# Frame axes read from a PSUM bank, three-term sums by tensor_reduce, and features stored component by component in a graph network's tensor product

## The chip, the core and the metric

The kernel runs on one core of a Trainium2 chip. The metric is the device time of one execution in microseconds (us); lower is better. Before the change the median of three runs is 9208.38 us (9191.51 to 9210.93).

## What is computed

Two message-passing layers run over one graph of 12,500 nodes and 400,000 edges (sorted by destination). The first is an attention layer with 4 heads. The second, which the change touches, is a tensor product. Each node has 32 features: 8 scalars and 8 vectors of 3 components.

```python
h = jnp.maximum(_layernorm(x, axis=-1), 0.0)
x = x + _L0_gnn_ref(h, Wq, Wk, Wv, Wo, edge_index)         # attention over edges
h = jnp.maximum(_layernorm(x, axis=-1), 0.0)
x = x + _L1_gnn_ref(h, edge_weight, edge_attr_3, edge_index, w1, b1, w2, b2)
# inside _L1_gnn_ref
R = jax.nn.relu(abs_distances[:, None] @ w1 + b1) @ w2 + b2   # 64 hidden units
Fj = features[src]                                            # one row of 32 per edge
acc = acc + _NORM[i] * jnp.einsum('euv,ef,evi,ofi->euo', Rb[..., k], Yf, Fb, C)
out = out.at[dst].add(msg)
```

## The kernel before

The kernel does not form the spherical harmonics. For each edge it keeps a frame: 3 axes of 3 numbers, the first along the edge. The three vector components of the gathered features are rotated into this frame, the radial products are formed there, and the result is rotated back.

The edges lie as 128 partitions by 3,132 slots. `tensor_product` walks over them in 58 chunks of T = 54 slots (`CHUNKS`, `T`), two buffers by turns. A chunk is cut into 9 steps (`SPC`, index s). The five engines run hand-written queues, tied by semaphores.

- GpSimd (POOL) issues 54 indirect DMAs for each chunk (L909). Each fetches 128 rows of `h2` (printed as `scratch_h`) into `feat[b]`. Its queue holds nothing else. It waits for `feat_free`, and two buffers are free at the start.
- TensorE makes the radial weights in `psR` (L924 and L925, six PSUM banks) and adds up the products over j by identity matmuls into `psS` (L935 and L938, two banks by turns). In its queue the radial matmuls of step s + 1 stand ahead of the sums of step s.
- VectorE (DVE) runs the order written in `body`: in step s come `products` (two instructions, L1181), then the pieces listed in `before` (of the last chunk's `finish`) and `ahead` (of the next chunk's `components`), then in steps 2, 5 and 8 a `split` (L1144), then `fold` (L1190).
- ScalarE (ACT) moves each step's sums from `psS` to `red` (L1027), and between those it does the hidden layer, copies of the scalars, the flags and the output.
- SyncE (SP) loads weights, stacked halves and frames.

```python
before = {1: (0, 1), 2: (2,), 3: (3, 4), 4: (5, 6)}
ahead = {5: (0,), 6: (1, 2), 7: (3,), 8: (4,)}
```

`components` rotates in. Its parts 0 to 2 multiply `feat` (vector components at steps of 3 words) by the frame (L1155, 1,296 elements each). Parts 3 and 4 add the three terms in two instructions (L1166 and L1168). Part 0 is where VectorE waits for a chunk's features. `finish` rotates back: three products (L1198), one addition (L1206), one addition that writes the transposed `seed` (L1210), and two scans along the edges (L1219). Ahead of the tensor product, `node_attention` writes `h2`; after it, `node_sums` gathers the sums of the nodes (L1292) and adds them to `x` (L1324). The first layer, `attention`, has a gather loop of the same make (L483), with its running state in PSUM tiles.

## Time and profile before

| what | value |
|---|---|
| median of three runs | 9208.38 us (9191.51 to 9210.93) |
| the profiled execution | 9176.9 us, its span 9175.1 us |
| busy, TensorE / VectorE / ScalarE / GpSimd | 42% / 55% / 21% / 75% of the span |
| stage of the tensor product | from about 4414 us to about 9035 us |

A busy share is an average over stages; the second half of the span, from about 4414 us, is the stage that is changed. In it TensorE and VectorE are busier than these shares say. A printed duration is from start to end; where instructions of VectorE follow each other at once, each starts about 0.08 us before the printed end of the one ahead.

### The profile page before, as it was taken

The numbers are of one execution on the slowest core, as the hardware profiler recorded it, in microseconds if no ns is written. First come the engines' busy times: TensorE is split into PE (matmuls) and PEld (weight loads), VectorE is DVE, ScalarE is ACT, GpSimd is POOL, SyncE is SP. The second block draws the span as 40 slices with busy tenths as digits, with TensorE's granted clock in tenths as the row PEclk, the third lists the DMA queues.
The fourth block names the chain that finished last, engine by engine and source line by source line (L and its number), as shares of the span: only waits on it lengthen the run. The fifth ranks groups of instructions, "written<-read, shape, count | busy, mean of one in ns | idle before, by whom it ended". The sixth has DMA issues, their size and how long they took to land. (4 is left out here: it accounts for less than half of the span.)

```text
span 9175.1 us, 70106 instructions
## 1 busy us (share of the span) xinstructions
PE 3812.2 (42%) x20406; PEld 2991.3 (33%) x20406; DVE 5008.3 (55%) x4743; ACT 1961.5 (21%) x1940; POOL 6926.4 (75%) x6677
## 2 busy tenths in 40 slices
PE   1000000000000000000388888888888888888883
PEld 0000000000000000000266666666666666666662
DVE  3133333333333333332477777777777777777773
ACT  0021221212212112121122222222222222222220
POOL 6777777777777777776777777777777777777774
PEclk6555555555555555555699999999999999999996
DMA  7122222222222222221233333333333333333331
GB/s 284 39 65 57 62 63 60 65 57 62 63 58 67 57 62 63 58 66 38 65 84 83 80 84 81 84 84 84 80 82 85 85 84 82 80 84 84 83 79 29
DMA packets 416998, 691.52 MB, mean 75 GB/s; under 512 B 170350, under 2 KB 247902, under 8 KB 405070
## 3 DMA queue, kind: packets, MB, share of 16 engines
q1 hardware_dynamic: 174376, 356.79, 14.4%
q0 software_dynamic: 213216, 166.16, 11.1%
q10 hardware_dynamic: 29382, 168.33, 4.5%
q14 instruction: 19, 0.16, 0.0%
q8 instruction: 5, 0.08, 0.0%
HBM read 345.81 MB, written 190.98 MB: 59 GB/s over the span
## 5 line engine op out<-in xcount | busy, mean ns | idle before, releaser
L909 POOL DMA_INDIRECT feat<-scratch_h,src x3132 | 3557.5, 1136 | 973.1 <-issue 954.2
L483 POOL DMA_INDIRECT kv<-scratch_kv,src_i x3132 | 2961.8, 946 | 968.0 <-issue 954.2
L935 PE MATMUL psS<-prod,ident 128*128 128x192 f32 x11136 | 1895.0, 326 | 0.0
L1181 DVE TENSOR_TENSOR prod<-psR,ops 128x1536 f32<-128x1536 f32 x1044 | 1784.6, 1752 | 148.4 <-PE psR L925 138.4
L935 PEld LDWEIGHTS psS<-prod,ident 128*128 128x128 f32 x11136 | 1838.6, 190 | 75.1 <-DVE prod L1181 0.3
L700 PE MATMUL psA<-ident,tail 128*36 128x128 f32 x3 | 0.8, 413 | 4098.9 <-DVEq L725 4098.9
L700 PEld LDWEIGHTS psA<-ident,tail 128*36 128x36 f32 x3 | 0.3, 128 | 4099.5 <-DVEq L725 4099.5
L924 PE MATMUL psR<-whigh,stack 128*128 128x512 f16 x3132 | 1227.9, 392 | 54.0 <-DVE prod L1181 36.3
L925 PE MATMUL psR<-wlow,capped 128*128 128x512 f16 x3132 | 1221.2, 390 | 0.0
L589 DVE TENSOR_TENSOR qk<-psQ,kv 128x1728 f32<-128x1728 f32 x58 | 113.5, 1957 | 2017.8 <-DMA kv<-scratch_kv,src_i 2017.8
L1027 ACT ACTIVATE red<-psS,scales 128x192 f32<-128x192 f32 x522 | 219.4, 420 | 3350.0 <-PE psS L938 3350.0
L938 PE MATMUL psS<-prod,ident 128*128 128x192 f32 x2784 | 603.3, 354 | 767.2 <-DVE prod L1190 767.2
L1155 DVE TENSOR_TENSOR parts<-feat,frame 128x1296 f32<-128x1296 f32 x174 | 329.8, 1924 | 923.8 <-DMA feat<-scratch_h,src 923.8
L938 PEld LDWEIGHTS psS<-prod,ident 128*128 128x128 f32 x2784 | 511.2, 207 | 784.0 <-DVE prod L1190 784.0
L509 ACT ACTIVATE psD<-decay 128x1980 f32<-128x1980 f32 x58 | 107.4, 1851 | 2588.6 <-DVEq L600 2588.6
L924 PEld LDWEIGHTS psR<-whigh,stack 128*128 128x128 f16 x3132 | 316.8, 101 | 398.2 <-issue 61.0
L925 PEld LDWEIGHTS psR<-wlow,capped 128*128 128x128 f16 x3132 | 315.4, 101 | 364.3 <-issue 46.4
L1190 DVE TENSOR_TENSOR prod<-prod 128x576 f32<-128x576 f32 x522 | 357.1, 684 | 2.2
L516 ACT ACTIVATE out<-sums 128x1944 f32<-128x1944 f32 x58 | 220.2, 3796 | 462.6 <-DVEq L608 462.6
L603 DVE TENSOR_TENSOR ev<-kv,psQ 128x1728 f32<-128x1728 f32 x58 | 178.2, 3072 | 151.3 <-ACT psQ L513 151.3
L1198 DVE TENSOR_TENSOR parts<-red,frame 128x1296 f32<-128x1296 f32 x174 | 256.9, 1503 | 6.2 <-ACT red L1027 6.2
L607 DVE TENSOR_TENSOR_SCAN sums<-psD,ev 128x1980 f32<-128x1980 f32 x58 | 248.3, 4281 | 2.0
(250 smaller groups left out, 3863.8 us busy)
## 6 DMA issues: line engine op xcount, KB each, us to landing
units<-in_wT SPq DMA_DIRECT2D x348, 288.0 KB, 4.6
scratch_state<-out ACTq DMA_DIRECT2D x58, 1080.0 KB
scratch_qexp<-zeros ACTq DMA_DIRECT2D x32, 1566.0 KB, 43.9
kv<-scratch_kv,src_i POOLq DMA_INDIRECT x3132
qin<-scratch_qexp SPq DMA_DIRECT2D x58, 864.0 KB, 4.6
feat<-scratch_h,src POOLq DMA_INDIRECT x3132
stack<-high SPq DMA_DIRECT2D x348, 144.0 KB
stack<-low SPq DMA_DIRECT2D x348, 144.0 KB
```

What stands on the lines that cost most here:

```text
L483: nc.gpsimd.indirect_dma_start(kv[b][:, t, :], None, a["kv"], bass.IndirectOffsetOnAxis(ap=src_i[b][:, t:t + 1].bitcast(U32), axis=0)).the ...
L516: nc.scalar.activation(out[b][:, :, 0:SUMS], sums[:, :, 1:T1].rearrange("p c t -> p t c"), ACT.Copy).then_inc(sums_copied, 1)
L607: step(v.tensor_tensor_scan(flat(sums), flat(decay_c), ev[:, :, :, :].rearrange("p h c t -> p (h c t)"), 0.0, ALU.mult, ALU.add))
L909: nc.gpsimd.indirect_dma_start(feat[b][:, t, :], None, a["h2"], bass.IndirectOffsetOnAxis(ap=src_i[b][:, t:t + 1].bitcast(U32), axis=0)).t ...
L924: nc.tensor.matmul(psR[:, g % 2, t, :], stack[:, slot, at:at + P], whigh[:, :], start=True, stop=False)
L925: last_mm = nc.tensor.matmul(psR[:, g % 2, t, :], capped[:, slot, at:at + P], wlow[:, :], start=False, stop=True)
L935: nc.tensor.matmul(psS[:, r, 0:GC].rearrange("p (x u) -> p x u", u=VU), ident[:, :], prod[r][:, :, j, :], start=(n == 0), stop=False)
L938: last_mm = nc.tensor.matmul(psS[:, r, 0:GC].rearrange("p (x u) -> p x u", u=VU), ident[:, :], prod[r][:, :, j, :], start=False, stop=(j = ...
L1155: step(v.tensor_tensor(parts[:, :, n, :].rearrange("p t (i v) -> p t i v", i=3), feat[b][:, :, VU:D].rearrange("p t (v i) -> p t i v", i=3 ...
L1181: v.tensor_tensor(prod[r][:, half * TRI * KINDS:(half + 1) * TRI * KINDS, :, :], psR[:, g % 2, :, :].rearrange("p t (x j u) -> p (t x) j u ...
L1190: v.tensor_tensor(prod[r][:, :, 0:FOLDS[s], :], prod[r][:, :, 0:FOLDS[s], :], prod[r][:, :, JC // 2:JC // 2 + FOLDS[s], :], ALU.add).then_ ...
L1198: step(v.tensor_tensor(parts[:, :, n, :].rearrange("p t (o u) -> p t o u", o=3), red[b][:, :, (n + 1) * VU:(n + 2) * VU].rearrange("p t (o ...
```

## The change

1. In `tensor_product`, ScalarE copies the frame of a chunk into a PSUM bank `psF` (486 elements) before each use: once for `components` (after the step-4 move of sums) and once for `finish` (after the step-0 move). VectorE reads the frame from there, and two semaphores (`axes_ready`, `axes_read`) hand the bank back and forth. The bank is taken from `psS`, which has one bank instead of two; TensorE's sums of a step now wait until ScalarE has moved those of the step ahead.
2. The three terms are added by `tensor_reduce`: in `components` three of them (1,296 elements read, 432 written each) in place of L1166 and L1168, in `finish` one (3,888 read, 1,296 written) in place of L1206 and L1210.
3. The vector features are stored component by component (i, then u) in `h2`, the sums and `state2`. `node_attention` makes a turned copy of its features for that, and `node_sums` adds in two instructions, one of them with a turned reading.

```diff
-        hs = sb("hs3", [P, BLOCKS, D])
+        hs, turned_hs = sb("hs3", [P, BLOCKS, D]), sb("turned_hs3", [P, BLOCKS, D])
...
-                                 hs[:, b0:b0 + blocks_of(i), :]).then_inc(h_stored, 16)
+                                 turned_hs[:, b0:b0 + blocks_of(i), :]).then_inc(h_stored, 16)
...
+                    step(v.tensor_copy(turned_hs[:, at, 0:VU], hs[:, at, 0:VU]))
+                    step(v.tensor_copy(turned_hs[:, at, VU:D].rearrange("p b (i u) -> p b u i", i=3),
+                                       hs[:, at, VU:D].rearrange("p b (u i) -> p b u i", i=3)))
...
-        psS = pb("psS", [P, 2, 512])
+        psS = pb("psS", [P, 512])
+        psF = pb("psF", [P, 512])
+        axes = psF[:, 0:9 * T].rearrange("p (t n i) -> p t n i", n=3, i=3)
...
+        axes_ready, axes_read = sem("axes_ready"), sem("axes_read")
...
-                    pe.wait_ge(sum_free, q + 1)
+                    pe.wait_ge(sum_free, q + 2)
...
+                def show_axes(b, copies, last_use):
+
+                    act.wait_ge(axes_read, copies)
+                    nc.scalar.activation(psF[:, 0:9 * T], frame[b][:, :, :].rearrange("p t c -> p (t c)"), ACT.Copy).then_inc(axes_ready, 1)
+                    if last_use:
+                        act.wait_ge(axes_ready, copies + 1)
+                        act.sem_inc(frame_free, 1)
...
+                act.wait_ge(frame_here[0], 16)
+                nc.scalar.activation(psF[:, 0:9 * T], frame[0][:, :, :].rearrange("p t c -> p (t c)"), ACT.Copy).then_inc(axes_ready, 1)
...
                             if s == 0 and not (first and b == 0):
+                                show_axes(1 - b, c * 2, True)
                                 seed_scalars(1 - b, c - 1)
+                            if s == 4 and more:
+                                act.wait_ge(frame_here[1 - b], (c + b) * 8 + 16)
+                                show_axes(1 - b, c * 2 + 1, False)
                             if s == 5 and not (first and b == 0):
                                 store(c - 1, at - T)
                             if s == 5:
...
+                show_axes(1, CHUNKS * 2 - 1, True)
                 seed_scalars(1, CHUNKS - 1)
...
-                def components(step, b, c, n):
-
+                def components(step, b, c, n, copies):
+
+                    def add_up(n):
+                        return v.tensor_reduce(ops[b][:, :, n + 1, VU:JC], parts[:, :, n, :].rearrange("p t (i u) -> p t u i", i=3), axis=AX.X, op=ALU.add)
                     if n < 3:
                         if n == 0:
                             vec.wait_ge(feat_here[b], (c - b) * (8 * T) + 16 * T)
-                            vec.wait_ge(frame_here[b], (c - b) * 8 + 16)
-                        step(v.tensor_tensor(parts[:, :, n, :].rearrange("p t (i v) -> p t i v", i=3),
-                                             feat[b][:, :, VU:D].rearrange("p t (v i) -> p t i v", i=3),
-                                             frame[b][:, :, 3 * n:3 * n + 3].rearrange("p t (i o) -> p t i o", o=1).to_broadcast([P, T, 3, VU]), ALU.mult), hold=False)
+                            vec.wait_ge(axes_ready, copies)
+                        step(v.tensor_tensor(parts[:, :, n, :].rearrange("p t (i u) -> p t i u", i=3),
+                                             feat[b][:, :, VU:D].rearrange("p t (i u) -> p t i u", i=3),
+                                             axes[:, :, n, :].rearrange("p t (i o) -> p t i o", o=1).to_broadcast([P, T, 3, VU]), ALU.mult), hold=False)
                         return
                     step.settle()
                     if n == 3:
+                        vec.sem_inc(axes_read, 1)
                         vec.wait_ge(ops_copied, c + 1)
                         vec.sem_inc(feat_free, 1)
-                    term = lambda i: parts[:, :, :, i * VU:(i + 1) * VU]
-                    to = ops[b][:, :, 1:KINDS, VU:JC]
-                    if n == 3:
-                        step(v.tensor_tensor(term(0), term(0), term(1), ALU.add), hold=False)
+                        step(add_up(0), hold=False)
+                        step(add_up(1), hold=False)
                     else:
-                        v.tensor_tensor(to, term(0), term(2), ALU.add).then_inc(turned_ready, 1)
+                        add_up(2).then_inc(turned_ready, 1)
...
-                def finish(step, b, c, n):
+                def finish(step, b, c, n, copies):

                     flat = lambda x, lo, hi: x[:, lo:hi, :].rearrange("p c t -> p (c t)")
                     if n < 3:
                         if n == 0:
                             vec.wait_ge(sum_free, c * SPC + SPC + 2)
+                            vec.wait_ge(axes_ready, copies)
                         step(v.tensor_tensor(parts[:, :, n, :].rearrange("p t (o u) -> p t o u", o=3),
                                              red[b][:, :, (n + 1) * VU:(n + 2) * VU].rearrange("p t (o u) -> p t o u", o=1).to_broadcast([P, T, 3, VU]),
-                                             frame[b][:, :, 3 * n:3 * n + 3].rearrange("p t (i o) -> p t i o", o=1).to_broadcast([P, T, 3, VU]), ALU.mult), hold=False)
+                                             axes[:, :, n, :].rearrange("p t (i o) -> p t i o", o=1).to_broadcast([P, T, 3, VU]), ALU.mult), hold=False)
                         return
                     step.settle()
                     if n == 3:
-                        vec.sem_inc(frame_free, 1)
+                        vec.sem_inc(axes_read, 1)
                         vec.sem_inc(red_free, 1)
-                        step(v.tensor_tensor(parts[:, :, 0, :], parts[:, :, 0, :], parts[:, :, 1, :], ALU.add), hold=False)
                     elif n == 4:
                         vec.wait_ge(scanned, c * 2 + 1)
                         step(v.tensor_copy(seed[:, :, 0], run[:, :, T]), hold=False)
-                        step(v.tensor_tensor(seed[:, VU:D, 1:T1].rearrange("p (u o) t -> p t o u", o=3),
-                                             parts[:, :, 0, :].rearrange("p t (o u) -> p t o u", o=3),
-                                             parts[:, :, 2, :].rearrange("p t (o u) -> p t o u", o=3), ALU.add), hold=False)
+                        step(v.tensor_reduce(seed[:, VU:D, 1:T1].rearrange("p x t -> p t x"),
+                                             parts[:, :, :, :].rearrange("p t n x -> p t x n"), axis=AX.X, op=ALU.add), hold=False)
...
-                of_finish = 6
+                of_finish = 5
...
-                                 state[:, b0:b0 + blocks_of(i), :]).then_inc(x_stored, 16)
+                                 k["res"][:, b0:b0 + blocks_of(i), :]).then_inc(x_stored, 16)
...
-                    step(v.tensor_tensor(state[:, at, :], state[:, at, :], k["res"][:, at, :], ALU.add))
+                    step(v.tensor_tensor(k["res"][:, at, 0:VU], k["res"][:, at, 0:VU], state[:, at, 0:VU], ALU.add))
+                    step(v.tensor_tensor(k["res"][:, at, VU:D].rearrange("p b (u o) -> p b u o", o=3),
+                                         k["res"][:, at, VU:D].rearrange("p b (u o) -> p b u o", o=3),
+                                         state[:, at, VU:D].rearrange("p b (o u) -> p b u o", o=3), ALU.add))
```

## Rows read from the trace of the kernel before

**Rows 1.** The page, section 1: engine, busy us, share of the span, instructions.
```profile
PE 3812.2 (42%) x20406; PEld 2991.3 (33%) x20406; DVE 5008.3 (55%) x4743; ACT 1961.5 (21%) x1940; POOL 6926.4 (75%) x6677
```

**Rows 2.** Busy time by window: PE, PEld, DVE, ACT, POOL, then clock, DMA share, GB/s.
```profile
6000.00:7000.00 1000.00, 825.34 (x4437) 649.58 (x4436) 765.41 (x549) 245.12 (x280) 788.53 (x694) 0.91 0.35 83
...
6045.30:6103.00 57.70, 57.51 (x312) 45.59 (x313) 55.55 (x40) 18.82 (x21) 45.43 (x41) 0.98 0.37 90
```

**Rows 3.** Groups by line on POOL, whole span: busy us, mean ns, idle before, releasers.
```profile
L909 POOL DMA_INDIRECT feat<-scratch_h,src x3132 | 3557.5, 1136 | 973.1 <-issue 954.2 <-DMA src<-in_src 18.9
L483 POOL DMA_INDIRECT kv<-scratch_kv,src_i x3132 | 2961.8, 946 | 968.0 <-issue 954.2 <-DMA src_i<-in_src 13.8
```

**Rows 4.** Waits of VectorE, 4700 to 8900 us (54 chunks): total us, times, longest.
```profile
DVE parts L1155 <- DMA feat<-scratch_h,src: 850.1, 54, 17.3
DVE prod L1181 <- PE psR L925: 112.5, 108, 2.0
```

**Rows 5.** Timeline of POOL and VectorE in step 6: start, duration in us.
```profile
6048.18 0.94 POOL L909 DMA_INDIRECT feat<-scratch_h,src  x1 [0.30 <-issue]
6048.48 3.80 DVE L1155 TENSOR_TENSOR parts<-feat,frame 128x1296 f32<-128x1296 f32 x2
6049.43 1.79 POOL L909 DMA_INDIRECT feat<-scratch_h,src  x1 [0.30 <-issue]
6051.52 1.55 POOL L909 DMA_INDIRECT feat<-scratch_h,src  x1 [0.30 <-issue]
...
6052.84 3.43 DVE L1181 TENSOR_TENSOR prod<-psR,ops 128x1536 f32<-128x1536 f32 x2
6053.38 0.95 POOL L909 DMA_INDIRECT feat<-scratch_h,src  x1 [0.30 <-issue]
```

**Rows 6.** Timeline of step 8 of another chunk.
```profile
4889.29 1.50 DVE L1168 TENSOR_TENSOR ops<-parts 128x1296 f32<-128x1296 f32 x1
4889.66 3.89 POOL L909 DMA_INDIRECT feat<-scratch_h,src  x1 [0.30 <-issue]
...
4890.70 1.36 DVE L1144 TENSOR_TENSOR low<-units,high 128x1152 f16<-128x1152 f32 x1
...
4891.97 0.76 DVE L1190 TENSOR_TENSOR prod<-prod 128x576 f32<-128x576 f32 x1
```

**Rows 7.** Groups by line, VectorE in the tensor product, whole span.
```profile
L1181 DVE TENSOR_TENSOR prod<-psR,ops 128x1536 f32<-128x1536 f32 x1044 | 1784.6, 1752 | 148.4 <-PE psR L925 138.4 <-ACT ops L989 5.8
L1155 DVE TENSOR_TENSOR parts<-feat,frame 128x1296 f32<-128x1296 f32 x174 | 329.8, 1924 | 923.8 <-DMA feat<-scratch_h,src 923.8
L1198 DVE TENSOR_TENSOR parts<-red,frame 128x1296 f32<-128x1296 f32 x174 | 256.9, 1503 | 6.2 <-ACT red L1027 6.2
L1144 DVE TENSOR_TENSOR low<-units,high 128x1152 f16<-128x1152 f32 x174 | 234.8, 1350 | 12.1 <-ACT high L976 12.0
L1219 DVE TENSOR_TENSOR_SCAN run<-same_c,seed 128x880 f32<-128x880 f32 x116 | 224.2, 1975 | 0.0
L1210 DVE TENSOR_TENSOR seed<-parts 128x1296 f32<-128x1296 f32 x58 | 142.5, 2457 | 0.0
L1166 DVE TENSOR_TENSOR parts<-parts 128x1296 f32<-128x1296 f32 x58 | 87.3, 1505 | 0.2 <-DVE parts L1155 0.2
```

**Rows 8.** Groups by line, VectorE in the attention stage, whole span.
```profile
L603 DVE TENSOR_TENSOR ev<-kv,psQ 128x1728 f32<-128x1728 f32 x58 | 178.2, 3072 | 151.3 <-ACT psQ L513 151.3
...
L589 DVE TENSOR_TENSOR qk<-psQ,kv 128x1728 f32<-128x1728 f32 x58 | 113.5, 1957 | 2017.8 <-DMA kv<-scratch_kv,src_i 2017.8
L591 DVE TENSOR_REDUCE score<-qk 128x216 f32<-128x1728 f32 x58 | 113.3, 1953 | 2.0
```

**Rows 9.** Timeline of VectorE and ScalarE in steps 0 and 1 of a chunk.
```profile
6073.84 2.92 DVE L1198 TENSOR_TENSOR parts<-red,frame 128x1296 f32<-128x1296 f32 x2
...
6076.02 0.42 ACT L1027 ACTIVATE red<-psS,scales 128x192 f32<-128x192 f32 x1 [6.39 <-PE psS L938]
6076.16 0.35 ACTq L1030 DMA_DIRECT2D src<-in_src  x1
...
6076.73 0.98 ACT L995 ACTIVATE seed<-red 128x432 f32<-128x432 f32 x1 [0.29 <-ACT red L1027]
```

**Rows 10.** Timeline of VectorE after the last features and at the end.
```profile
8927.40 1.89 DVE L1155 TENSOR_TENSOR parts<-feat,frame 128x1296 f32<-128x1296 f32 x1 [15.88 <-DMA feat<-scratch_h,src]
...
9015.74 4.34 DVE L1198 TENSOR_TENSOR parts<-red,frame 128x1296 f32<-128x1296 f32 x3 [6.24 <-ACT red L1027]
...
9168.13 0.76 DVE L1324 TENSOR_TENSOR state<-state,res 128x576 f32<-128x576 f32 x1 [22.26 <-DMA state<-scratch_state,last_i]
```

More of the change, by code:

```diff
@@ L934, in sums @@
                     for n, j in enumerate(order):
-                        nc.tensor.matmul(psS[:, r, 0:GC].rearrange("p (x u) -> p x u", u=VU), ident[:, :], prod[r][:, :, j, :], start=(n == 0), stop=False)
+                        nc.tensor.matmul(psS[:, 0:GC].rearrange("p (x u) -> p x u", u=VU), ident[:, :], prod[r][:, :, j, :], start=(n == 0), stop=False)
                     pe.wait_ge(prod_ready, q + 1)
                     for j in range(FOLDS[s]):
-                        last_mm = nc.tensor.matmul(psS[:, r, 0:GC].rearrange("p (x u) -> p x u", u=VU), ident[:, :], prod[r][:, :, j, :], start=False, stop=(j == FOLDS[s] - 1))
+                        last_mm = nc.tensor.matmul(psS[:, 0:GC].rearrange("p (x u) -> p x u", u=VU), ident[:, :], prod[r][:, :, j, :], start=False, stop=(j == FOLDS[s] - 1))
                     last_mm.then_inc(sum_ready, 1)
@@ L943, in _ @@
                 for j in range(4):
-                    turn = nc.tensor.matmul(psS[0:1, 0, j * P:(j + 1) * P], tops[:, j:j + 1], ident[:, :], start=True, stop=True)
+                    turn = nc.tensor.matmul(psS[0:1, j * P:(j + 1) * P], tops[:, j:j + 1], ident[:, :], start=True, stop=True)
                 turn.then_inc(tops_turned, 1)
                 pe.wait_ge(scales_ready, 1)
-                nc.tensor.matmul(psS[:, 1, 0:4], ones_row[:, :], scales0[:, :], start=True, stop=True).then_inc(scales_spread, 1)
+                nc.tensor.matmul(psS[:, 0:4], ones_row[:, :], scales0[:, :], start=True, stop=True).then_inc(scales_spread, 1)
                 pe.wait_ge(wrad_ready, 1)
@@ L1094, in _ @@
                 at0 = lambda n: tops0[:, n:n + 1]
[L1095 to L1097 removed]
+                step(v.tensor_reduce(tops0[:, 0:3], psS[0:1, 0:3 * P].rearrange("p (j n) -> p j n", j=3), axis=AX.X, op=ALU.max))
+                step(v.tensor_reduce(at0(3), psS[0:1, 3 * P:3 * P + HID], axis=AX.X, op=ALU.max))
+                step(v.tensor_copy(at0(4), psS[0:1, 3 * P + HID:3 * P + HID + 1]))
                 def power_of_two(x):
@@ L1119, in _ @@
                 vec.wait_ge(scales_spread, 1)
-                step(v.tensor_copy(scales[:, :], psS[:, 1, 0:4]))
+                step(v.tensor_copy(scales[:, :], psS[:, 0:4]))
                 step(v.tensor_scalar(w1[:, :], w1[:, :], scales[:, 0:1], None, ALU.mult))
@@ L1248, in _ @@
                 for n in range(7):
-                    finish(step, 1, CHUNKS - 1, n)
+                    finish(step, 1, CHUNKS - 1, n, CHUNKS * 2)
                 vec.wait_ge(run_copied, CHUNKS + 1)
```

11 lines of the change are left out of this document (4 added, 7 removed).

## The prediction

> **What bounds the kernel now.** I read the busy shares first, then the windows, the waits, and last the timeline of two engines side by side.
>
> Over the whole span GpSimd is the busiest engine [rows 1]. Inside the tensor product all of the big three look near full: GpSimd 79%, TensorE 83%, VectorE 77% [rows 2]. The waits decide. Once in every chunk VectorE waits for the gathered features, 850.1 us in 54 chunks, which is 15.7 us each; for TensorE it waits 2.1 us a chunk [rows 4]. GpSimd waits for nobody: its idle time is "issue", 0.305 us ahead of each gather (954.2 / 3132) [rows 3]. So the chunk lasts as long as its 54 gathers: 54 x (1.136 + 0.305) = 77.8 us, and the rest of a chunk's work takes 77.8 - 15.7 = 62.1 us. TensorE is the second limit: between two waits for features it is busy 57.51 of 57.70 us [rows 2].
>
> A gather costs 1.136 us here, and one of the same make 0.946 us in the attention stage [rows 3]. The timeline shows why. A gather takes 0.94 us when it starts ahead of L1155, 1.79 and 1.55 us when it starts inside it, and 0.95 us inside L1181 [rows 5]. L1155 has two inputs in SBUF; L1181 has one in SBUF and one in PSUM. The stretched gathers end about 0.87 us after the end of the VectorE instruction in which they start. In the attention stage VectorE runs L589 and L603 (one input in PSUM) and L591 (a tensor_reduce, one input), and the gathers there stay at 0.946 us on average [rows 3, 8]. The waste is 1.136 - 0.946 = 0.190 us a gather, 10.3 us a chunk.
>
> **The change part by part.**
>
> *Gathers that no longer stretch.* Ten of the instructions with two SBUF inputs go in each chunk: three L1155, L1166, L1168, three L1198, L1206 and L1210 [rows 7]. Three L1144, nine L1190 and two L1219 stay. I price a run of them so: a gather comes every 1.25 us (0.946 + 0.305) and is held from its start inside the run to the end of the instruction. An instruction of L us that is longer than 1.25 catches one gather, for L - 0.62 on average; the next one comes 1.25 after its release, so a second instruction right behind costs its length less 1.25, or nothing; a short one alone costs L x L / 2.5. Lengths are the row's less the 0.08 us of overlap.
>
> Tried on the kernel before, by steps: 5 (1.84, 1.27, 0.67) 1.2; 6 (1.84, 1.84, 0.67) 1.8; 7 (1.42, 0.48) 0.8; 8 (1.42, 1.27, 0.67) 0.8; 0 (0.67) 0.2; 1 (1.42, 1.42, 0.48) 1.0; 2 (1.42, 1.27, 0.67) 0.8; 3 (1.42, then 2.38) 2.1; 4 (1.90, 1.90, 0.48) 1.9. Sum 10.6, against 10.3 measured. What stays after the change: L1144 in three steps 0.65 each, 1.95; folds alone 3 x 0.18 + 2 x 0.09 = 0.7; the scans 1.9. Sum 4.6, scaled by 10.3 / 10.6 it is 4.5 us a chunk. Gain 5.8 us a chunk; the period of the gathers becomes 67.5 + 4.5 = 72.0 us.
>
> Bounds: the holds depend on where gathers fall, and each instruction catches one for between L - 1.25 and L. That gives 1.4 us (L1144 0.02 x 3, scans 2 x 0.65) and 9.3 us (L1144 3.8, folds 3.0, scans 2.5). One row warns upward: a gather that starts in L1168 takes 3.89 us, through L1144 and L1190 to the end of the third [rows 6]. If L1144 with its fold did that in three steps, 2 us more. The Trainium skill ("SBUF — State Buffer", Who interferes with whom) says that a VectorE instruction with two SBUF inputs contends with a GpSimd instruction that reads SBUF, and one with at most one does not. The trace agrees on which instructions hold a gather; by its rule alone, one hold for one instruction, the 3.89 us gather would have ended after about 1.9 us.
>
> *VectorE's own time.* The three L1155 fall from 1.92 to about 1.48 us, since feat is read in one stretch and L1181 shows 1.14 ns an element with an operand in PSUM (1752 / 1536): 1.3 us saved [rows 7]. L1198 stays at 1.50. The reduces read 3 x 1296 and 3888 elements. Contiguous, as in L591, an element costs 1.13 ns (1953 / 1728); read at a large step in SBUF, as kv in L603, 1.78 ns (3072 / 1728), and L589 shows that the PSUM operand is not to blame, 1.13 ns with PSUM at a step [rows 8]. Here the terms lie 8 and 24 words apart, so I take L603: three reduces at 2.3 us for the 3.0 us of L1166 and L1168, +3.9; one at 6.9 for the 3.96 us of L1206 and L1210, +3.0. By L591 it would be +1.4 and +0.4. An upper bound is L1210, which writes at a large step: 2457 / 1296 = 1.90 ns, together 0.9 us more [rows 7]. The Trainium skill ("SBUF — State Buffer", Door 1: The DMA port swizzle) has 16-byte lines and a penalty for every access that crosses into a new one, which speaks against these reduces; it names no price, and the trace agrees (L603 against L591).
>
> *The new waits.* In step 1 VectorE starts L1198 at 6073.84, while ScalarE moves the step-0 sums only at 6076.02 [rows 9]. The copy of the axes is queued behind that move and a DMA issue, and takes about 0.6 us (estimate: between 0.42 us for 192 elements and 0.98 us for 432 [rows 9]). So VectorE stands until about 6077.1: 3.3 us, and fold, products and scans queue behind it. It has 2.1 us of waits for TensorE a chunk that this absorbs in part. In step 4 the copy comes about a microsecond before VectorE's need; if late it costs tenths. The single psS bank: TensorE's next sums come 2.6 us after the last, behind 12 radial matmuls, and ScalarE's move takes 0.42 us, so nothing; in step 6 ScalarE is busy with the output, but ready by then. The copies also cover frame_free, which SP waits for a chunk ahead: nothing.
>
> So the chain beside the gathers grows from 62.1 to at most 62.1 - 1.3 + 3.9 + 3.0 + 3.3 = 71.0 us (71.9 by L1210), to about 69 if the old 2.1 us absorb the new wait, and to 65.9 if the reduces read at full rate. All stand under 72.0: the gathers still bound, by a thin margin, and VectorE's wait for features shrinks to 1 to 6 us. That wait is the cover; with it gone each microsecond on VectorE costs 57.
>
> *The ends.* From 8927.40 no gather runs, and VectorE and TensorE set the time to the end of the stage [rows 10]. The chain of the last full chunk is about 5 us longer, and the last finish takes one reduce of 6.9 for 3.9 and one exposed copy of axes, 0.6. With the turned copies ahead (about 1 us of the last turn) and the second addition at the very end (0.3 beside 0.76 us [rows 10]): +10 us together. Chunks with VectorE work beside gathers are 57.
>
> Sum: 57 x 5.8 = 331, less 10, gives 321 us. The profiled execution took 9176.9, the median of the runs 9208.38, 31.5 us more; I take the same gap on both sides: 8856 for a profile, 8887 us for the median, -3.5%.
>
> **The rivals.**
>
> 1. *The rest holds less than I priced.* Phases lock, since VectorE restarts with a gather each chunk. At the lower bound of 1.4 us the gathers take 68.9 and the 69 us chain binds: 9208 + 10 - 57 x 8.8 = 8717 us.
> 2. *VectorE becomes the bound.* Reduces at 1.90 ns, the whole 3.3 us wait and some more in step 4, or gathers held through L1144 and L1190: period 74 to 77. At 75.5: 9208 + 10 - 57 x 2.3 = 9087 us. For it: the margin above is about 1 us. Against: it needs two of the bounds.
> 3. *The other side, slower: the strided reduce.* If it read at more than L603's rate, the period would pass 77.8 when the chain has 6.8 us more than 71.0 over 7776 elements, that is at 1.78 + 0.87 = 2.65 ns. At 3 ns: 57 x 2.7 + 10 = +164, 9372 us. No row reaches 2 ns.
> 4. *No change of the gathers.* If the reduces held gathers as the old pieces did, only L1155 and L1198 would stop: steps 5, 6, 1 and 2 of the sum above lose 3.2 us a chunk, 9208 + 10 - 57 x 3.2 = 9036 us. L591 speaks against it [rows 8].
>
> **How the numbers follow.** Forecast (period 70 to 74) 0.62; rival 1 0.14; rival 2 0.13; rival 3 0.05; rival 4 0.04; nothing in it within 0.2% 0.02. A run within 0.2% of 9208 could not be told from no change. Forecast 8887, its own range 8770 to 9000; with the near parts of rivals 1, 2 and 4 I give 8760 to 9020. Faster 0.93, same 0.02, slower 0.05.
>
> **What would show it.** L909 at a mean near 1.03 us, still with only issue gaps; no gather over 1.0 us that starts in L1155, L1198 or a reduce; the reduces at 2.3 and 6.9 us (or 1.5 and 4.4); VectorE's wait for features 1 to 6 us a chunk, a new wait of 2 to 3 us for ACT's copy ahead of L1198. Wrong if GpSimd starts to wait for feat_free (then VectorE binds), or if L909's mean stays above 1.1.

## The result, and the profile after

The changed kernel takes 8865.49 us (median of four runs, 8863.89 to 8867.84); the kernel before took 9205.09 us in four runs beside it. The ratio is 0.9636, 95% interval 0.9622 to 0.9649: 3.6% faster. Forecast were 8887 us and a range of 8760 to 9020.

The page's busy line and the window 6000 to 7000 us of the kernel after, with the columns of [rows 1, 2]:

```profile
PE 3847.8 (43%) x20406; PEld 2975.6 (34%) x20406; DVE 5077.3 (57%) x4758; ACT 2022.8 (23%) x2056; POOL 6614.8 (75%) x6677
```

```profile
6000.00:7000.00 1000.00, 900.67 (x4806) 699.26 (x4806) 839.88 (x595) 280.20 (x332) 772.32 (x748) 0.95 0.37 90
```

GpSimd's busy time falls by 312 us with the same 6,677 instructions [rows 1]. TensorE and VectorE have almost the old busy time in total, and more of it in each millisecond [rows 2]. The groups on GpSimd show the place, with those of [rows 3]:

```profile
L915 POOL DMA_INDIRECT feat<-scratch_h,src x3132 | 3241.6, 1035 | 974.0 <-issue 954.3 <-DMA src<-in_src 19.7
L483 POOL DMA_INDIRECT kv<-scratch_kv,src_i x3132 | 2967.0, 947 | 967.9 <-issue 954.1 <-DMA src_i<-in_src 13.8
```

The gathers of the tensor product have a mean of 1035 ns in place of 1136; the gaps between them and the gathers of the attention stage are as before. Busy and idle time of the group, over 58 chunks, give the period of a chunk: (3557.5 + 973.1) / 58 = 78.1 us before, (3241.6 + 974.0) / 58 = 72.7 us after. The difference over the stage, 315.0 us, against 309.1 us between the two spans leaves 5.9 us for everything outside it. Where these lie can be read from the first and the last gather of the stage, before and after:

```profile
4414.35 0.94 POOL L909 DMA_INDIRECT feat<-scratch_h,src  x1 [18.95 <-DMA src<-in_src]
8925.03 0.94 POOL L909 DMA_INDIRECT feat<-scratch_h,src  x1 [0.30 <-issue]
```

```profile
4421.48 0.95 POOL L915 DMA_INDIRECT feat<-scratch_h,src  x1 [19.74 <-DMA src<-in_src]
8616.40 0.94 POOL L915 DMA_INDIRECT feat<-scratch_h,src  x1 [0.30 <-issue]
```

From the first of them to the end of the last it takes 4511.6 us before and 4195.9 after, 315.7 less (the sums above also hold some 19 us of waiting ahead of the first). What follows it takes 249.1 us before and 248.7 us after. What stands ahead of it is 7.1 us longer, and 6.1 of these lie in the attention stage, whose last gather ends at 4232.9 before and at 4239.0 after. No edit touches that stage, and in five other kernels of the experiments its last gather ends between 4233.3 and 4235.6, so most of this is a difference between executions.

The waits of VectorE in the kernel after, from 4700 to 8600 us (54 chunks), to be held against [rows 4]:

```profile
DVE parts L1178 <- DMA feat<-scratch_h,src: 406.5, 54, 8.6
DVE parts L1221 <- ACT psF L987: 179.4, 54, 3.4
DVE prod L1203 <- PE psR L931: 32.0, 53, 1.3
```

VectorE still waits for the features once a chunk, 7.5 us in place of 15.7, and once for the copy of the axes, 3.3 us. GpSimd still waits for nobody. So the same engine sets the period, and each chunk lost 5.4 us of its time.

The groups of VectorE in the kernel after, with those of [rows 7]:

```profile
L1203 DVE TENSOR_TENSOR prod<-psR,ops 128x1536 f32<-128x1536 f32 x1044 | 1782.3, 1748 | 53.4 <-PE psR L931 51.5 <-ACT ops L1003 1.7
L1212 DVE TENSOR_TENSOR prod<-prod 128x576 f32<-128x576 f32 x522 | 356.0, 682 | 2.2
L1173 DVE TENSOR_REDUCE ops<-parts 128x432 f32<-128x1296 f32 x174 | 277.9, 1624 | 0.3 <-DVE parts L1178 0.3
L1232 DVE TENSOR_REDUCE seed<-parts 128x1296 f32<-128x3888 f32 x58 | 262.0, 4517 | 0.0
L1221 DVE TENSOR_TENSOR parts<-red,psF 128x1296 f32<-128x1296 f32 x174 | 255.7, 1498 | 196.6 <-ACT psF L987 196.6
L1178 DVE TENSOR_TENSOR parts<-feat,psF 128x1296 f32<-128x1296 f32 x174 | 255.7, 1497 | 462.5 <-DMA feat<-scratch_h,src 462.5
...
L1165 DVE TENSOR_TENSOR low<-units,high 128x1152 f16<-128x1152 f32 x174 | 234.6, 1349 | 11.8 <-ACT high L982 11.6
L1240 DVE TENSOR_TENSOR_SCAN run<-same_c,seed 128x880 f32<-128x880 f32 x116 | 224.1, 1974 | 0.0
```

The products of the rotation in (L1178) take 1497 ns in place of 1924, those of the rotation back are unchanged, and the reduces take 1624 and 4517 ns: 1.25 ns and 1.16 ns for each element read.

Two stretches of the timeline of the kernel after, POOL and VectorE, show which instructions hold a gather now. The first is step 8:

```profile
6031.30 1.62 DVE L1173 TENSOR_REDUCE ops<-parts 128x432 f32<-128x1296 f32 x1
6032.29 0.95 POOL L915 DMA_INDIRECT feat<-scratch_h,src  x1 [0.30 <-issue]
6032.84 1.34 DVE L1165 TENSOR_TENSOR low<-units,high 128x1152 f16<-128x1152 f32 x1
6033.54 2.13 POOL L915 DMA_INDIRECT feat<-scratch_h,src  x1 [0.30 <-issue]
6034.11 0.75 DVE L1212 TENSOR_TENSOR prod<-prod 128x576 f32<-128x576 f32 x1
...
6059.83 4.52 DVE L1232 TENSOR_REDUCE seed<-parts 128x1296 f32<-128x3888 f32 x1
6060.69 0.95 POOL L915 DMA_INDIRECT feat<-scratch_h,src  x1 [0.30 <-issue]
6061.95 0.94 POOL L915 DMA_INDIRECT feat<-scratch_h,src  x1 [0.30 <-issue]
```

A gather inside a reduce takes its 0.95 us. The one that starts in the split L1165 takes 2.13 us and ends at 6035.67, which is 0.81 us after the end of the fold L1212 behind the split (6034.86): it was held through both.

I sorted the gathers from 4700 to 8600 us by the VectorE instruction in which each starts, and added up what each held one takes over 0.941 us (the unheld ones' mean). The entries are good to about 0.1 us. The same was done for the kernel before and for the experiments below, whose names stand in the head; us a chunk:

| starts in | before | after | layout only | SBUF frame | two-input adds | early axes | more reduces |
|---|---|---|---|---|---|---|---|
| products, rotating in | 2.28 | 0 | 0.94 | 1.23 | 0 | 0 | 0 |
| additions, rotating in | 3.37 | 0 | 0.68 | 0 | 1.33 | 0 | 0 |
| products, rotating back | 0.92 | 0 | 1.20 | 1.23 | 0 | 0 | 0 |
| additions, rotating back | 2.20 | 0 | 2.30 | 0 | 1.81 | 0 | 0 |
| splits | 0 | 1.98 | 0 | 1.84 | 0.66 | 2.16 | 2.17 |
| folds | 0.35 | 0.95 | 0.11 | 0.95 | 0.18 | 0.40 | 0.84 |
| scans | 1.51 | 2.05 | 1.53 | 2.04 | 1.53 | 1.73 | 2.02 |
| sum | 10.6 | 5.0 | 6.8 | 7.3 | 5.5 | 4.3 | 5.0 |

The change took 8.8 us of holds away, and 3.1 us came back at splits, folds and scans, which it did not touch.

### The profile page after: what moved, and what is told of

Read it like the earlier page. It is cut to its first block and busy times, and to the rows that moved or that the text cites. A ratio compares the mean times of both kernels' runs of the same rounds, so it can differ in the third digit from the quotient of the medians.

```text
span 8866.0 us, 70608 instructions
## 1 busy us (share of the span) xinstructions
PE 3847.8 (43%) x20406; PEld 2975.6 (34%) x20406; DVE 5077.3 (57%) x4758; ACT 2022.8 (23%) x2056; POOL 6614.8 (75%) x6677
## 5 line engine op out<-in xcount | busy, mean ns | idle before, releaser
L915 POOL DMA_INDIRECT feat<-scratch_h,src x3132 | 3241.6, 1035 | 974.0 <-issue 954.3
L1178 DVE TENSOR_TENSOR parts<-feat,psF 128x1296 f32<-128x1296 f32 x174 | 255.7, 1497 | 462.5 <-DMA feat<-scratch_h,src 462.5
L930 PEld LDWEIGHTS psR<-whigh,stack 128*128 128x128 f16 x3132 | 315.0, 101 | 497.6 <-DVE prod L1203 164.7
L1221 DVE TENSOR_TENSOR parts<-red,psF 128x1296 f32<-128x1296 f32 x174 | 255.7, 1498 | 196.6 <-ACT psF L987 196.6
L1212 DVE TENSOR_TENSOR prod<-prod 128x576 f32<-128x576 f32 x522 | 356.0, 682 | 2.2
L1173 DVE TENSOR_REDUCE ops<-parts 128x432 f32<-128x1296 f32 x174 | 277.9, 1624 | 0.3 <-DVE parts L1178 0.3
L603 DVE TENSOR_TENSOR ev<-kv,psQ 128x1728 f32<-128x1728 f32 x58 | 178.0, 3070 | 151.3 <-ACT psQ L513 151.3
```

The lines of the kernel that those rows point to most:

```text
L915: nc.gpsimd.indirect_dma_start(feat[b][:, t, :], None, a["h2"], bass.IndirectOffsetOnAxis(ap=src_i[b][:, t:t + 1].bitcast(U32), axis=0)).t ...
L930: nc.tensor.matmul(psR[:, g % 2, t, :], stack[:, slot, at:at + P], whigh[:, :], start=True, stop=False)
L1173: return v.tensor_reduce(ops[b][:, :, n + 1, VU:JC], parts[:, :, n, :].rearrange("p t (i u) -> p t u i", i=3), axis=AX.X, op=ALU.add)
L1178: step(v.tensor_tensor(parts[:, :, n, :].rearrange("p t (i u) -> p t i u", i=3), feat[b][:, :, VU:D].rearrange("p t (i u) -> p t i u", i=3 ...
L1212: v.tensor_tensor(prod[r][:, :, 0:FOLDS[s], :], prod[r][:, :, 0:FOLDS[s], :], prod[r][:, :, JC // 2:JC // 2 + FOLDS[s], :], ALU.add).then_ ...
L1221: step(v.tensor_tensor(parts[:, :, n, :].rearrange("p t (o u) -> p t o u", o=3), red[b][:, :, (n + 1) * VU:(n + 2) * VU].rearrange("p t (o ...
```

## The experiments

The theory throughout: the time is that of the gathers, and what counts of each edit is how it changes their holds. The four kernels that come first ran on one chip, where the kernel before took 9180.53 us; at the ratio above, the kernel after would take about 8846 us there (8833 to 8858 by the ratio's interval). It was not itself run there, so the spans of the profiled executions (8866.0 us for the kernel after) and the gathers' periods are given too, and are the closer measure.

**The frame left in SBUF.** The kernel after, with all six products of a chunk reading the frame in SBUF; the same edit stands in both lines of products. The copies to the bank are still made and still waited for; the frame's buffer is given back by VectorE after its last product instead of by ScalarE.

```diff
-                                             axes[:, :, n, :].rearrange("p t (i o) -> p t i o", o=1).to_broadcast([P, T, 3, VU]), ALU.mult), hold=False)
+                                             frame[b][:, :, 3 * n:3 * n + 3].rearrange("p t (i o) -> p t i o", o=1).to_broadcast([P, T, 3, VU]), ALU.mult), hold=False)
```

> The changed kernel, but the six products of a chunk read the frame from SBUF again (the copies to PSUM and their waits stay). Theory (gathers bound, held by VectorE instructions with two SBUF inputs): by the pricing of the prediction the holds grow by 0.15 + 0.8 + 0.9 + 0.15 = 2.0 us a chunk, 57 x 2.0 = +114 us on 8865: about 8980, mean gather 1.035 -> 1.07 us. Rival (what counted was VectorE's own time or the reduces): L1178 and L1221 keep their length, so no change, 8865.

Measured: 8985.74 us, ratio 0.9786 (0.977 to 0.9802). The gathers' group, and, from 4700 to 8600 us, the two groups that now have two inputs in SBUF:

```profile
L915 POOL DMA_INDIRECT feat<-scratch_h,src x3132 | 3369.6, 1076 | 973.8 <-issue 954.1 <-DMA src<-in_src 19.6
```

```profile
L1175 DVE TENSOR_TENSOR parts<-feat,frame 128x1296 f32<-128x1296 f32 x159 | 235.4, 1508 | 496.3 <-DMA feat<-scratch_h,src 496.3
...
L1218 DVE TENSOR_TENSOR parts<-red,frame 128x1296 f32<-128x1296 f32 x156 | 230.5, 1505 | 172.4 <-ACT psF L987 172.4
```

The products take 1508 and 1505 ns, as with the bank (1497, 1498), yet the kernel is slower, by 140 us by the ratios and by 123 us by the spans (8989.3 us). So the bank is worth nothing to VectorE's own time and 2.2 us a chunk to the gathers (period 74.9 against 72.7), which is some 126 us. The timeline of this kernel shows the hold:

```profile
5090.88 2.92 DVE L1175 TENSOR_TENSOR parts<-feat,frame 128x1296 f32<-128x1296 f32 x2
5091.84 1.36 POOL L915 DMA_INDIRECT feat<-scratch_h,src  x1 [0.30 <-issue]
5093.50 1.11 POOL L915 DMA_INDIRECT feat<-scratch_h,src  x1 [0.30 <-issue]
```

**Two-input additions in place of the reduces.** The kernel after, with the additions of the kernel before.

```diff
-                        step(add_up(0), hold=False)
-                        step(add_up(1), hold=False)
+                        step(v.tensor_tensor(term(0), term(0), term(1), ALU.add), hold=False)
...
-                        add_up(2).then_inc(turned_ready, 1)
+                        v.tensor_tensor(ops[b][:, :, 1:KINDS, VU:JC], term(0), term(2), ALU.add).then_inc(turned_ready, 1)
...
+                        step(v.tensor_tensor(parts[:, :, 0, :], parts[:, :, 0, :], parts[:, :, 1, :], ALU.add), hold=False)
...
-                        step(v.tensor_reduce(seed[:, VU:D, 1:T1].rearrange("p x t -> p t x"),
-                                             parts[:, :, :, :].rearrange("p t n x -> p t x n"), axis=AX.X, op=ALU.add), hold=False)
+                        step(v.tensor_tensor(seed[:, VU:D, 1:T1].rearrange("p x t -> p t x"),
+                                             parts[:, :, 0, :], parts[:, :, 2, :], ALU.add), hold=False)
```

> The changed kernel with the additions as two-input instructions again (two in the rotation in, two in the rotation back), frame still in PSUM. Theory: holds of 0.8 for 0.1 in step 7, 0.8 for 0.65 in step 8, 2.1 for 0.2 in step 3: +2.75 us a chunk, 57 x 2.75 = +157: 9022, mean gather about 1.085; up to 9120 if the gather of step 8 is again carried through three instructions as in the kernel before. Rival (VectorE's own time binds): the additions take 1.9 + 0.1 us less than the reduces, so slightly faster, 8865 or down to 8750.

Measured: 8887.71 us, ratio 0.9681 (0.9665 to 0.9698), so only some 41 us above the kernel after by the ratios, and 23 us by the spans (8889.4 us). This is a miss of mine. The gathers' group:

```profile
L915 POOL DMA_INDIRECT feat<-scratch_h,src x3132 | 3268.2, 1043 | 973.9 <-issue 954.2 <-DMA src<-in_src 19.7
```

The additions do hold gathers, 3.1 us a chunk in the table; but splits, folds and scans hold 2.6 us less, since the gathers now come at other moments in them. The holds of neighbouring instructions can't be added up one by one.

**The layout alone.** The kernel before, with the features stored component by component (part 3 of the change, with its turned copies and the addition in two instructions), and nothing else. The two edits inside the chunk are:

```diff
-                                             feat[b][:, :, VU:D].rearrange("p t (v i) -> p t i v", i=3),
+                                             feat[b][:, :, VU:D].rearrange("p t (i v) -> p t i v", i=3),
...
-                        step(v.tensor_tensor(seed[:, VU:D, 1:T1].rearrange("p (u o) t -> p t o u", o=3),
+                        step(v.tensor_tensor(seed[:, VU:D, 1:T1].rearrange("p (o u) t -> p t o u", o=3),
```

> The kernel before with the features stored component by component and nothing else (frame in SBUF, two-input additions, two psS banks). Theory: L1155 falls from 1.92 to 1.50 us, so its holds shrink, 0.4 in step 5 and 0.8 in step 6: -1.2 us a chunk, -70 us: about 9135. Rival (layout matters only on VectorE, which waits anyway): 9205.

Measured: 8961.29 us, ratio 0.9764 (0.9747 to 0.978): 219 us, two thirds of the whole gain, and far more than expected. Groups of this kernel, on POOL over the whole span and on VectorE from 4700 to 8600 us:

```profile
L912 POOL DMA_INDIRECT feat<-scratch_h,src x3132 | 3340.3, 1066 | 973.8 <-issue 954.2 <-DMA src<-in_src 19.7
```

```profile
L1158 DVE TENSOR_TENSOR parts<-feat,frame 128x1296 f32<-128x1296 f32 x159 | 235.8, 1510 | 640.6 <-DMA feat<-scratch_h,src 640.6
```

The three shorter products (1510 ns for 1924) hold 1.3 us less, which I had counted in. What I had not is the addition in step 8. Its timeline in this kernel answers to [rows 6]:

```profile
5097.60 1.50 DVE L1171 TENSOR_TENSOR ops<-parts 128x1296 f32<-128x1296 f32 x1
5098.74 1.17 POOL L912 DMA_INDIRECT feat<-scratch_h,src  x1 [0.30 <-issue]
5099.01 1.35 DVE L1147 TENSOR_TENSOR low<-units,high 128x1152 f16<-128x1152 f32 x1
5100.22 0.96 POOL L912 DMA_INDIRECT feat<-scratch_h,src  x1 [0.30 <-issue]
5100.28 0.75 DVE L1193 TENSOR_TENSOR prod<-prod 128x576 f32<-128x576 f32 x1
```

In the kernel before, a gather started 0.37 us into this addition and was held through three instructions, 3.89 us. That was no single case: in 47 of its chunks a gather starts 0.36 to 0.41 us in and takes 3.87 to 3.89 us. Here the gather starts 1.14 us in and takes 1.17 us, and in no chunk is one that starts in this addition held past its end. The same three instructions stand behind each other; what has moved is the moment: VectorE starts afresh with each chunk's features, the shorter products bring it to step 8 about 1.2 us sooner, and the gathers ahead of step 8 are held less as well. That this is what moved the moment is worked out from the lengths and not tested by itself.

**The axes copied earlier.** The kernel after, with one thing moved: ScalarE's copy for the rotation back stands ahead of its wait for step 0's sums instead of behind it.

```diff
+                            if s == 0 and not (first and b == 0):
+                                show_axes(1 - b, c * 2, True)
...
                             if s == 0 and not (first and b == 0):
-                                show_axes(1 - b, c * 2, True)
                                 seed_scalars(1 - b, c - 1)
```

> The changed kernel with the copy of the axes for the rotation back put ahead of the wait for the step-0 sums, so that VectorE's 3.3 us wait for it goes. Theory (gathers bound): the wait moves into the wait for features (7.5 -> about 10.8 us a chunk), the time stays within 10 us of 8865. Rival (the new wait is on the path): 57 x 3.3 = -188, 8677.

Measured: 8817.99 us, ratio 0.9607 (0.9591 to 0.9624), the fastest of all. Waits of VectorE in the same stretch, and the gathers' group:

```profile
DVE parts L1179 <- DMA feat<-scratch_h,src: 459.1, 54, 8.6
...
DVE prod L1204 <- PE psR L931: 108.8, 109, 1.7
```

```profile
L915 POOL DMA_INDIRECT feat<-scratch_h,src x3132 | 3197.1, 1021 | 973.8 <-issue 954.1 <-DMA src<-in_src 19.7
```

The wait of 3.3 us is gone. It did not shorten the chunk by 3.3: 1 us of it turned up in the wait for the features (8.5 for 7.5), 1.4 us in waits for TensorE (2.0 for 0.6). The gain is some 28 us by the ratios and 50 by the two spans (8866.0 and 8816.4), and is all in the gathers' mean: 1021 against 1035 ns is 44 us over 3,132 of them; folds and scans hold less after the shift (0.40 and 1.73 us a chunk for 0.95 and 2.05). Neither number I gave was right.

**More work for VectorE.** The kernel after, with the three reduces of the rotation in done a second time into a tile that nothing reads.

```diff
+                        for m in range(2):
+                            step(v.tensor_reduce(spare[:, m, :, :], parts[:, :, m, :].rearrange("p t (i u) -> p t u i", i=3), axis=AX.X, op=ALU.add), hold=False)
```

> The kernel after with each of the three reduces of a chunk done a second time into a spare tile that nothing reads: VectorE has about 1.6 + 4.5 us more a chunk (the rows of the kernel after give 1624 and 4517 ns), that is 7.7 us with the second reduce of step 1. Theory (VectorE's chain of some 65 us lies inside a period of 72.4 us that POOL's gathers set, so the added time comes out of the wait for the features, 7.5 us a chunk in the kernel after): the wait falls to 0 to 2 us, the ratio stays at 0.959 to 0.972. Rival (VectorE's time lies on the path in full): plus 6 to 8 us a chunk, ratio 0.998 to 1.01.

The expectation is wrong on the work added: the reduce of the rotation back is not among the three, so that it is 3 x 1.63 less the overlaps, 4.6 us a chunk, and not 7.7. The rival then says 0.992. (So it stood in the expectation of the first run of this kernel, with 0.959 to 0.968 by the theory; that run comes below.) Measured, on a chip where the kernel before took 9178.69 us: 8867.62 us, ratio 0.9658 (0.9642 to 0.9674). Gathers and waits of this kernel:

```profile
L916 POOL DMA_INDIRECT feat<-scratch_h,src x3132 | 3240.5, 1035 | 974.0 <-issue 954.4 <-DMA src<-in_src 19.7
```

```profile
DVE parts L1179 <- DMA feat<-scratch_h,src: 217.7, 54, 4.4
DVE parts L1225 <- ACT psF L988: 156.0, 54, 3.0
```

The window from 6000 to 7000 us has VectorE busy for 902.18 us against 839.88. All of it came out of waits: for the features 4.0 us a chunk in place of 7.5, the rest out of the waits for the copy and for TensorE. The gathers' mean stays at 1035 and the span at 8864.0 us (8866.0 in the kernel after). Time added to VectorE costs nothing as long as the wait for the features covers it, and the reduces hold no gather: 171 gathers start in the extra ones, and none takes over 0.95 us.

**Runs on chips where ScalarE stands.** The remaining kernels ran on chips on which the kernel before itself took 10,836 to 11,217 us: there ScalarE stands for tens of microseconds at a time, and GpSimd and TensorE wait behind it. The profile calls such a release "remote": it finds no instruction of this core that gave it. More than ScalarE is slower there. In the attention stage, which no edit touches, the gathers take 1051 to 1053 ns for 946 in all of these runs, and TensorE too has idle time with no releaser. The ratios of these runs decide nothing on the holds.

With the splits of steps 2 and 5 moved behind the scans and the axes copied early:

```diff
-                            if s % 3 == 2 and not (last and b == 1):
-                                split(i, (b + 1) * PACKS + s // 3)
+                            if not (last and b == 1):
+                                for pack in {4: (0, 1), 8: (2,)}.get(s, ()):
+                                    split(i, (b + 1) * PACKS + pack)
```

> The kernel after with two things moved and no work added: the copy of the axes for the last step ahead of the wait for step 0's sums, and the frame's split of steps 2 and 5 behind the scans of step 4 instead of ahead of TensorE's rows. Theory (what is left of the stretch is set by where a gather happens to start in a run of two-input instructions): the splits' 2.16 us of hold a chunk fall to about 0.8 us, so that the ratio to the kernel before comes to about 0.952 to 0.956 and the mean of L915's gathers to about 1.00 us. Rival (the holds only change their place: the 2 us come back at the scans): ratio 0.960 as with the early copy alone, mean 1.02 us. The kernel's first run stood on a chip that was disturbed throughout and says nothing on this.

Measured: 12376.83 us beside 10836.36, ratio 1.1398; in a first run of the same kernel 12503.07 beside 11216.8, ratio 1.1211. The waits of ScalarE, GpSimd and TensorE over the span in the run that gave 1.1398 (those of ScalarE and GpSimd are 71 and 57, of 51 and 57 us each on average):

```profile
ACT red L1045 <- remote: 3626.6, 71, 71.5
POOL feat L915 <- DMA src<-in_src: 3246.6, 57, 61.0
PE psS L941 <- ACT red L1045: 1527.5, 36, 50.4
...
PE psS L941 <- issue: 876.0, 23, 48.3
```

The indices of the gathers are loaded by ScalarE's queue, so POOL stands with it. With one fold in each step on top (`FOLDS = (1, 1, 1) * PACKS` in place of `(3, 2, 3) * PACKS`):

> The kernel after with the copy of the axes ahead of the wait for step 0's sums, the frame's splits of steps 2 and 5 behind the scans of step 4, and each fold of TensorE's sums taken per product instead of once per pack (its tuple of folds at one each, so that TensorE adds about 4.9 us a chunk and VectorE's folds go). Theory (the period is the gathers' own time and the holds left; TensorE and VectorE have cover for it): the folds' 0.4 to 0.95 us and most of the splits' 2.16 us of hold go, the period comes to 70.4 to 71.2 us and the ratio to the kernel before to 0.950 to 0.955. Rival (TensorE's longer rows make the chain the bound): period 72.5 us or more and ratio 0.963 or above, with VectorE's wait for the features near zero.

Measured: 12713.17 us beside 10919.27, ratio 1.1667. The kernel with more reduces, in a first run on such a chip, took 12750.35 beside 11216.8, ratio 1.1426, where it gave 0.9658 above. So the same program is 3.4% faster than the kernel before on one chip and 14% slower on another. The kernel before with one `psS` bank instead of two took 11307.17 beside 11216.8, ratio 1.0164 (1.0055 to 1.0273):

> The kernel before with one psS bank for two, nothing else. Theory: TensorE's next sums stand 2.6 us of radial matmuls behind the last, ScalarE's move takes 0.42, so no wait: ratio 0.998 to 1.002. Rival (a hidden cost of the bank): up to 1 us a chunk on the chain, still under the wait for features, so also about 1.000, but a new wait of TensorE for ScalarE would show in the profile.

No wait was expected, and this run has one. TensorE stands for ScalarE's move of the sums:

```profile
PE psS L935 <- ACT red L1027: 638.4, 80, 35.8
```

The two runs on such chips that keep two banks (the next kernel) have no such wait, and the four runs with the change in them have 1527.5 to 2140.8 us of it. So where ScalarE stands, the single bank makes TensorE stand with it. These four took 12 to 17% longer than the kernel before beside them, and the three runs of kernels built on the kernel before lie at 0.98 to 1.02. The change as a whole may be a loss on such a chip; that isn't shown, since it was not run there.

On the undisturbed chip the page of the kernel after has 0.5 us of this wait in 11,136 matmuls:

```profile
L941 PE MATMUL psS<-prod,ident 128*128 128x192 f32 x11136 | 1895.1, 326 | 0.5 <-ACT red L1043 0.5
```

**A pause ahead of the addition of step 8.** One of these kernels tells something by its timeline. It is the kernel before with a memset of 480 elements of a spare tile ahead of L1168 (0.46 us), so that the addition starts later against the gathers.

```diff
+                        step(v.memset(spare[:, :], 0.0), hold=False)
                         v.tensor_tensor(to, term(0), term(2), ALU.add).then_inc(turned_ready, 1)
```

> The same kernel as e10_pause, whose first run fell where both kernels took over 11,000 us. The kernel before with a memset of 480 elements (about 0.5 us, no SBUF input) right ahead of L1168. Theory (it matters where a gather falls in a run of two-input instructions): the 3.9 us gather of step 8 goes, 57 x 2.2 = -125 us, ratio about 0.986. Rival (only the sum of the two-input time counts): ratio 1.000 to 1.003.

Measured: 10747.99 us beside 10935.87, ratio 0.9794 (0.972 to 0.9868): faster with more work. But a first run, on another such chip, gave 0.996 (0.9898 to 1.0023), and the two intervals don't meet, so the time shows nothing for certain. The timeline of the second run in step 8:

```profile
7057.41 0.46 DVE L1169 MEMSET spare<- 128x480 f32 x1
7057.78 1.44 DVE L1170 TENSOR_TENSOR ops<-parts 128x1296 f32<-128x1296 f32 x1
7058.28 1.76 POOL L910 DMA_INDIRECT feat<-scratch_h,src  x1 [0.30 <-issue]
7059.14 1.34 DVE L1145 TENSOR_TENSOR low<-units,high 128x1152 f16<-128x1152 f32 x1
7060.34 0.96 POOL L910 DMA_INDIRECT feat<-scratch_h,src  x1 [0.30 <-issue]
```

The gather starts 0.50 us in and is released at the end of the addition. Gathers above 3.5 us number 47 in the kernel before, on its undisturbed chip, and 9 and 10 in the two runs of this one, none of them in this addition. ScalarE's stalls shift the moments too, so the count supports the reading without proving it.

## Why the prediction was right, point by point

**What bounds it.** Right. GpSimd sets the period before and after: its idle time is issue gaps in all kernels of the undisturbed chips, and 4.6 us more work on VectorE a chunk left the gathers' mean at 1035 ns.

**The gathers that no longer stretch.** Right on which instructions hold a gather, and close in total: 4.5 us of holds were forecast to stay, 4.8 stayed by the same baseline (54 x (1.035 - 0.946)). The table has splits, folds and scans at 1.98, 0.95 and 2.05 where I had 1.95, 0.7 and 1.9. The period is 72.7 us for 72.0. No gather is held in L1178, L1221 or a reduce, as "what would show it" asked. That the total is so close is in part luck. In the kernel before the rule gave steps 7 and 8 1.6 us, and the additions there hold 3.4; it gave steps 1 and 2 1.8 us, and the products there hold 0.9 with nothing in the splits. On the share of each part it is weaker still: by it the layout was to bring 1.2 us a chunk (9135 us), and brought 3.7 (78.1 - 74.4); the reduces were to bring 2.75 and, once the other two parts are there, bring 0.5 (73.1 - 72.7, against the kernel with additions). It prices a gather's place as an average, while each chunk repeats the same places; over nine steps such errors largely cancelled, over one part they don't. The warning I had put to rows 6, held gathers carried through a split and its fold, did come true in one of the three splits, that of step 8: in 56 chunks the gather that starts 0.68 to 0.72 us into it takes 2.11 to 2.15 us. It stays inside the bound.

**VectorE's own time.** L1178 right (1.48 forecast, 1.497). The reduces are the term of the sum that was mis-sized: by L603's rate I took 2.3 and 6.9 us, they take 1.62 and 4.52, L591's rate (forecast as the lower end, 1.5 and 4.4). The step that failed is "the terms lie 8 and 24 words apart, so I take L603". L603 reads at a step of 64 words and repeats its other operand (`to_broadcast`); a step alone does not make a rate of 1.78 ns, and what does in L603 was not tested. The rule of the Trainium skill ("SBUF — State Buffer", Door 1: The DMA port swizzle), a penalty for each access to a new 16-byte line, which I had set against the reduces, is hardly borne out for them: reads at a step of 32 and of 96 bytes cost 1.25 and 1.16 ns, against 1.13 for the contiguous ones of L591.

So the chain beside the gathers is 72.7 - 7.5 = 65.2 us a chunk, where I had put 69 to 71 and 65.9 for reduces at full rate, and the wait for the features is 7.5 us and not 1 to 6. The margin that I called thin is wide. It had no effect on the time, because this chain is hidden.

**The new waits.** Right: 3.3 us forecast ahead of the rotation back, 3.3 measured; 0.6 us for the copy, 0.58 measured; nothing for the single bank, 0.5 us in all, on this chip; where ScalarE stands it is not nothing (638.4 us above). The old waits for TensorE fell from 112.5 to 32.0 us over the stretch, as the part that absorbs it.

**The ends.** Right in size by luck. 10 us were forecast, 9 of them behind the last features and 1 ahead of the first. Ahead, the gap between the last gather of the attention stage and the first of the tensor product grew by 1.1 us, as forecast. Behind, nothing was lost: up to the end of the last scans it takes 1.6 us more (113.4 us after the last gather for 111.8), and the sums of the nodes take 2.0 us less, in every kernel with the new layout; why was not looked into. What fills the 5.9 us is mainly the 6.1 us of the untouched attention stage. The step that was mis-sized is "the chain of the last full chunk is about 5 us longer, and the last finish takes one reduce of 6.9 for 3.9".

**The sum.** Over the stage 331 us were forecast to be gained, and 315.7 were; outside it, 10 to be lost, and 0.7 were, with 6.1 more in the attention stage. From the profile before: 9176.9 - 315.7 + 0.7 + 6.1 = 8868 us, and the profile after took 8867.84, with 8856 forecast. The 15 us that were missed at the gathers are partly hidden by the ends that didn't come. The medians then stand 31.5 us above the profile before and 2 us below it after, so that the gap I had added on both sides was chance: it is what makes the forecast of 8887 us lie above the 8865.49 measured.

**The rivals.** None came, though the premise of rival 1, that phases lock, holds: the same gather is held in the same step in chunk after chunk. It does not make the holds few. Its chain of 69 us and the rate of 1.90 ns in rival 2 were both out of the question with reduces at 1.16 to 1.25 ns. Rival 4 had the reduces hold gathers; none does. The Trainium skill ("SBUF — State Buffer", Who interferes with whom) says so of this instruction, that it never contends on this chip, and the timeline agrees: 0.94 to 0.95 us in L1232. The same section counts a VectorE instruction with two SBUF inputs as contending with a GpSimd instruction that reads SBUF, as the gather does (it reads its rows' numbers from `src`), and the experiment with the frame left in SBUF agrees: 2.2 us a chunk.

## What to carry to other kernels

When indirect gathers issued by GpSimd set the pace, look for VectorE instructions with both inputs in SBUF beside them, and move one input to PSUM or turn an addition of several terms into a reduce; beyond that, time on VectorE costs only what its wait for the gathers can't cover, and moves the moments at which gathers fall, for better or worse. Price such holds by the places where gathers fall, read from the timeline, and for all instructions of a chunk together. The parts don't add up, and a shift of a microsecond can be worth as much as the instruction removed (here the layout brought 3.7 us a chunk, the bank 2.2 and the reduces 0.5, the last two each measured with the rest in place). Treat a forecast of such a sum as good to a few us a chunk. Test a kernel whose sums, copies and index loads all hang on one engine's queue on more than one chip.

## What the runs showed that I had not expected

- A held gather is usually let go at the end of the instruction in which it starts (about 0.8 to 0.9 us are left then), but sometimes it is carried through the next ones: 3.89 us through three instructions when it starts 0.37 us into L1168 [rows 6], 2.13 us through two when it starts 0.70 us into L1165. The moment within the instruction does not decide alone: in the second run with the memset five gathers start 0.33 to 0.39 us into the addition, and each is let go at its end. What decides is open; no run varied the moment alone on an undisturbed chip.
- A tensor_reduce that reads SBUF at a step of 8 or 24 words runs at 1.25 or 1.16 ns an element, as the contiguous L591 does at 1.13. A product that reads the features at a step of 3 words loses more: 1924 ns against 1510 ns with the frame in SBUF in both.
- With the frame in PSUM or in SBUF the product takes the same time (1497 and 1508 ns): the whole worth of the bank lies on another engine.
- On four of the chips ScalarE stood again and again, for up to 85.1 us, and a kernel that is 3.4% faster elsewhere was 14% slower there. The profile names no releaser; the cause stays open, and the kernel after itself and the early copy were not run on such a chip.
